# Attention behind a feed-forward block: the last projections, maxima, splits and scales of a batch put at other places of its opening

## What is computed

```python
ckv   = x @ w_kv + b_kv                                   # latent, 128 wide
key   = concat([ckv @ w_ku + b_ku, x @ w_kr + b_kr])      # 256 + 256 wide
q_lat = x @ w_q + b_q
query = concat([q_lat @ w_qu + b_qu, q_lat @ w_qr + b_qr])
value = ckv @ w_vu + b_vu                                 # 512 wide
scores = einsum('bhqd,bhkd->bhqk', heads(query), heads(key))   # 16 heads of 32, causal
at  = softmax(scores / sqrt(32))
out = (at @ heads(value)) @ w_o + b_o
```

## Time and profile before

| | before |
|---|---|
| median of 3 runs | 1224.05 us (1222.79 to 1225.31) |
| the profiled execution, its own time | 1222.3 us |
| its span, first to last instruction | 1220.5 us |
| mean granted TensorE clock | 0.975 |
| TensorE matmuls busy | 1081.9 us (89%) |
| VectorE | 900.7 us (74%) |
| ScalarE | 803.6 us (66%) |
| GpSimd | 362.1 us (30%) |

### The profile page before, as it was taken

The page is one execution under the profiler, slowest core; times in us unless marked ns, Lnnn a source line. Parts: engine busy times, 40 slices in busy tenths (PEclk is TensorE's granted clock), DMA queues, the critical chain, the costliest instruction groups (busy, mean ns, idle before and its releaser), DMA issues.

```text
span 1220.5 us, 18032 instructions
## 1 busy us (share of the span) xinstructions
PE 1081.9 (89%) x5939; PEld 489.4 (40%) x5990; DVE 900.7 (74%) x2229; ACT 803.6 (66%) x1193; POOL 362.1 (30%) x388
## 2 busy tenths in 40 slices
PE   0788999998898789999999699999999799998886
PEld 0343455554444333332344233232344345554443
DVE  4788888989984888884335887884234798888893
ACT  5489888888645345666615355567547988888762
POOL 2101244444561342101210450002200133443456
PEclk9998999998999889999999899999999999999998
DMA  9200000002000221210000321100000000000000
GB/s 368 99 1 1 2 1 1 2 1 57 1 1 1 71 66 29 53 36 2 1 21 9 76 56 34 47 36 2 1 1 1 1 1 19 19 18 18 19 19 35
DMA packets 22287, 37.45 MB, mean 31 GB/s; under 512 B 5398, under 2 KB 7833, under 8 KB 21532
## 3 DMA queue, kind: packets, MB, share of 16 engines
q1 hardware_dynamic: 21404, 34.54, 9.0%
q0 software_dynamic: 768, 1.57, 0.5%
HBM read 19.17 MB, written 4.21 MB: 19 GB/s over the span
## 4 chain that ended last, share of the span: by engine, by line
PE 62%; DVE 21%; issue 7%; SPq 3%; POOL 2%; ACT 2%; DMA 1%; DVEq 1%; another core or an unknown queue 0%; POOLq 0%; ACTq 0%
PE zP L521 14%; PE oP L573 11%; PE xP L693 5%; PE oP L693 5%; PE zP L619 5%; PE zP L677 4%; PE hP L656 3%; PE hP L543 3%; DVE arena L1301 3%; DVE m L1309 3%; PE zP L718 2%; PE hP L718 2%; DVE scored L1506 2%; PE zP L656 2%; DVE arena L1382 1%
## 5 line engine op out<-in xcount | busy, mean ns | idle before, releaser
L834 ACT ACTIVATE arena<-arena,X 128x2048 int8<-128x2048 f32 x154 | 307.9, 2005 | 4.9 <-DVE X L1281 4.8
L893 ACT ACTIVATE arena<-zP,asc 128x512 f32<-128x512 f32 (+3 forms) x384 | 200.6, 582 | 108.2 <-PE zP L681 78.8
L521 PE MATMUL zP<-T,arena 128*128 128x512 f16 x1024 | 249.8, 388 | 0.9
L573 PE MATMUL oP<-T,arena 128*128 128x512 f16 x832 | 200.5, 385 | 0.9 <-DVE arena L1396 0.9
L521 PEld LDWEIGHTS zP<-T,arena 128*128 128x128 f16 x1024 | 102.3, 100 | 123.2 <-issue 12.1
L790 ACT ACTIVATE arena<-zP,sc 128x512 f32<-128x512 f32 x128 | 87.4, 687 | 93.8 <-PE zP L526 65.3
L573 PEld LDWEIGHTS oP<-T,arena 128*128 128x128 f16 x832 | 82.2, 99 | 79.6 <-issue 6.0
L677 PE MATMUL zP<-arena 98*128 98x512 f16 (+3 forms) x384 | 110.5, 334 | 2.6 <-DMA arena<-arena 1.7
L656 PE MATMUL hP<-arena 96*128 96x512 f16 (+3 forms) x256 | 84.0, 351 | 16.0 <-DVE mx L1506 12.9
L1010 POOL TENSOR_SCALAR ln<-ln 128x1 f32<-128x1 f32 x32 | 38.6, 1205 | 189.8 <-DVE ln L1221 189.6
L1506 DVE CUSTOM_DVE_ANT_0 scored<-hP,causal 128x128 bf16<-128x128 f32 (+3 forms) x170 | 80.6, 484 | 19.1 <-PE hP L656 17.8
(11 more groups left out here) (207 smaller groups left out, 1834.6 us busy)
## 6 DMA issues: line engine op xcount, KB each, us to landing
arena<-arena SPq DMA_DIRECT2D x168, 64.0 KB, 2.0
arena<-in_w_synT SPq DMA_DIRECT2D x4, 1024.0 KB, 8.1
arena<-in_w_outT SPq DMA_DIRECT2D x4, 1024.0 KB, 14.8
out_dram<-x_sb SPq DMA_DIRECT2D x16, 256.0 KB, 2.0
x_sb<-in_x SPq DMA_DIRECT2D x3, 1024.0 KB, 14.0
arena<-in_w_o SPq DMA_DIRECT2D x2, 1024.0 KB, 5.0
arena<-arena POOLq DMA_DIRECT2D x24, 64.0 KB, 1.9
arena<-in_b_syn SPq DMA_DIRECT2D x1, 1024.0 KB, 12.0
```

The costliest lines, as they stand in the source:

```text
L521: pe.matmul(zP[:, c * CW:(c + 1) * CW], part[:, g % 2, k, :], T1[:, k, c * CW:(c + 1) * CW], start=(n == 0 and k == 0), stop=False)
L573: mm = pe.matmul(o, part[:, k, :], T2[:, k, :], start=(c == 0 and n == 0 and k == 0), stop=False)
L834: act.activation(junk[:, counted[0] % 2, :], Z[:, g % ZR, :], ACT.Sign, bias=X[:, 2, k:k + 1], accum_out=S[:, k:k + 1]).then_inc(sm["cnt"], 1)
L893: act.activation(PT[:, m // 4 % 2, h, q0:512], colP[m % 3][:, q0:512], ACT.Exp, scale=asc[:, g, 10:11]).then_inc(sm["exp_done"], 1)
```

## The change

It changes the order of work in the opening of a batch. The "in" items for the key planes move forward in `ITEMS`; `project` ends after 14 items; items 14 to 27 stand in `ORDER`, items 14 to 19 among the rows of unit (0, 0) and the values behind them, among the rows of unit (0, 1) (`opening`, `behind_opening`). High halves ("hi"), plane maxima ("peak", with the scales of the group where they complete it) and low halves ("lo") become entries of `ORDER` too. The low halves 0 and 1 come with the first "in 2" item, now the ninth; 2 and 3 are in the opening, 4 to 7 behind eleven rows of unit (0, 1). GpSimd sets the units of stack 0 at the head of `project`, before the first `all_max`; those of stacks 1 and 2 stay. `load_stack` and SyncE's list stay as they are.

```diff
+def opening(rows):
+    order = [("hi", 1), ("item", 14)] + take(4) + [("peak", 14), ("item", 15), ("lo", 2)] + take(4) + [("lo", 3)]
+    order += [("item", 16), ("item", 17)] + take(2) + [("peak", 15), ("item", 18)] + take(2) + [("item", 19)] + take(4)
+    return order
+
+def behind_opening(rows, turn):
+    r = iter(rows)
+    order = [("item", 20), ("item", 21)]
+    for n in range(3):
+        order += [next(r)] + [("item", 22 + n)] * (n < 2)
+    order += [turn, ("item", 24), ("peak", 16), ("peak", 17), next(r), ("item", 25), next(r), ("item", 26), ("hi", 2)]
+    order += [next(r), ("item", 27), ("peak", 18), ("peak", 19), next(r), next(r), ("hi", 3)]
+    for n in range(3):
+        order.append(next(r))
+    for n in range(4):
+        order += [next(r), next(r), ("lo", 4 + n)]
+    return order + list(r)
...
-            others = [[("val", n)] + ([("lo", n + 3)] if 1 <= n <= 4 else []) for n in range(BT)]
-            unit = [e for n in range(BT) for e in others[n] + unit[2 * n:2 * n + 2]]
+            unit = opening(unit)
+        elif (g, qc) == (0, 1):
+            unit = behind_opening(unit, turn)
+            turn = None
...
-        start[u] = min(len(rows), rows.index(("turn", *u)) + 1 + LEAD)
+        lead = [n for n, e in enumerate(rows) if e[0] == "row" and n > rows.index(("turn", *u))]
+        start[u] = lead[LEAD - 1] + 1 if len(lead) >= LEAD else len(rows)
...
         ITEMS = [("in", j, tc) for tc in range(2) for j in (0, 1)]
-        ITEMS += [("up", j, tc) for j in (0, 2, 1, 3, 4, 5) for tc in range(2)]
-        ITEMS += [("in", j, tc) for j in (2, 3) for tc in range(2)]
-        VALUES = len(ITEMS)
+        for kind, j in (("up", 0), ("up", 2), ("in", 2), ("up", 1), ("up", 3), ("in", 3), ("up", 4), ("up", 5)):
+            ITEMS += [(kind, j, tc) for tc in range(2)]
+        assert len(ITEMS) == FIRST_VAL
...
                     evac_item(b, n)
-                    if n - 2 in COMPLETE:
-                        split_hi(b, COMPLETE.index(n - 2))
-                split_hi(b, 3)
+                    if ITEMS[n] == ("in", 2, 0):
+                        split_hi(b, 0)
...
-                            act.wait_ge(sm["p_ps"], (b + 1) * len(ITEMS))
+                            act.wait_ge(sm["p_ps"], b * len(ITEMS) + FIRST_VAL)
...
             def project(b):
+                pool.wait_ge(*((sm["a_rstd"], BT) if b else (sm["x_new"], NT)))
+                unit_rows(b, 0)
                 for g in range(GROUPS):
                     all_max(b, g)
...
             def core(b):
-                for g in range(3):
+                for g in (1, 2):
...
-                for n in range(VALUES):
-                    if not plane(ITEMS[n]):
-                        continue
-                    w, g, tc = plane(ITEMS[n])
+                for n in range(IN_CORE):
+                    if plane(ITEMS[n]):
+                        peak(b, n)
                     if ITEMS[n] == ("in", 2, 0):
-                        for m in range(4):
+                        for m in range(2):
                             split_lo(b, m)
```

More of the change, by code:

```diff
@@ L45, with take @@
 ATT_SCALE = 1.0 / HD ** 0.5
+IN_CORE = 14
+FIRST_VAL = 20
+def opening(rows):
+    r = iter(rows)
+    def take(n):
+        return [next(r) for _ in range(n)]
+    order = [("hi", 1), ("item", 14)] + take(4) + [("peak", 14), ("item", 15), ("lo", 2)] + take(4) + [("lo", 3)]
+    order += [("item", 16), ("item", 17)] + take(2) + [("peak", 15), ("item", 18)] + take(2) + [("item", 19)] + take(4)
+    return order
+def behind_opening(rows, turn):
+    r = iter(rows)
+    order = [("item", 20), ("item", 21)]
[8 more added lines that the diff above has]
+    return order + list(r)
 def core_order():
@@ L295, in program @@
         COMPLETE = [max(n for n, e in enumerate(ITEMS) if plane(e) and plane(e)[1] == g) for g in range(GROUPS)]
-        TOTAL = {k: seen(k, len(ORDER)) for k in ("row", "max", "turn", "col", "mix", "norm", "rec", "mix_v", "val", "lo")}
+        TOTAL = {k: seen(k, len(ORDER)) for k in ("row", "max", "turn", "col", "mix", "norm", "rec", "mix_v")}
         RING = [e for e in ORDER if e[0] in ("row", "turn")]
@@ L318, in x_bank @@
             return hP[:, 0, :] if (f, i) == (1, 0) else xP[:, :]
-        IN_DONE = max(n for n, e in enumerate(ITEMS) if e[0] == "in") + 1
         STACK_OF = (0, 1, 2, 0)
@@ L636, in core @@
                     kind, g = e[:2]
-                    stack = stacks[STACK_OF[g]] if g < GROUPS else None
+                    stack = stacks[STACK_OF[g]] if kind in ("row", "col") else None
                     if kind in ("row", "turn"):
@@ L641, in core @@
                             pe.wait_ge(*free)
[L642 to L645, removed]
+                    elif kind == "item":
+                        item(b, g)
+                    m = n.get(kind, 0)
+                    n[kind] = m + 1
                     if kind == "row":
@@ L878, in core @@
                     kind, g = e[:2]
-                    m = n[kind]
-                    n[kind] += 1
+                    m = n.get(kind, 0)
+                    n[kind] = m + 1
                     if kind in ("row", "turn"):
                         bank, _ = next(ring)
-                    if kind == "val":
-                        evac_item(b, VALUES + g)
+                    if kind == "item":
+                        evac_item(b, g)
+                    elif kind == "hi":
+                        split_hi(b, g)
                     if kind == "col":
@@ L1050, in project, with unit_rows @@
             def project(b):
+                pool.wait_ge(*((sm["a_rstd"], BT) if b else (sm["x_new"], NT)))
+                unit_rows(b, 0)
                 for g in range(GROUPS):
                     all_max(b, g)
+            def unit_rows(b, g):
+                pool.memset(stacks[g][3 * HD:3 * HD + 2, 1, :, :], MUNIT).then_inc(sm["unit_set"], 1)
+                pool.wait_ge(sm["unit_set"], 3 * b + g + 1)
             def all_max(b, g):
@@ L1068, in core @@
                         wait_stack(pool, b, 1)
-                    pool.memset(stacks[g][3 * HD:3 * HD + 2, 1, :, :], MUNIT).then_inc(sm["unit_set"], 1)
-                    pool.wait_ge(sm["unit_set"], 3 * b + g + 1)
+                    unit_rows(b, g)
                 pool.wait_ge(sm["bo_in"], 16 * (b + 1))
@@ L1454, in project, with peak @@
             def project(b):
-                for n in range(VALUES):
-                    if not plane(ITEMS[n]):
-                        continue
-                    w, g, tc = plane(ITEMS[n])
+                for n in range(IN_CORE):
+                    if plane(ITEMS[n]):
+                        peak(b, n)
                     if ITEMS[n] == ("in", 2, 0):
-                        for m in range(4):
+                        for m in range(2):
                             split_lo(b, m)
[L1462 to L1468, removed]
+            def peak(b, n):
+                w, g, tc = plane(ITEMS[n])
+                dve.wait_ge(sm["p_out"], b * len(ITEMS) + n + 1)
+                step(dve.tensor_reduce(mxq[:, g, w, tc:tc + 1], qk[:, w, g, tc * 512:(tc + 1) * 512],
+                                       AX.X, ALU.max, apply_absolute_value=True))
+                if n in COMPLETE:
+                    after(0)
+                    dve.tensor_reduce(asc[:, g, 0:2], mxq[:, g, :, :], AX.X, ALU.max).then_inc(sm["p_max"], 1)
+                    scale(b, g)
             def scale(b, g):
@@ L1498, in core @@
                         split_lo(b, g)
+                    elif kind == "peak":
+                        peak(b, g)
                     if kind == "row":
```

## The result

The changed kernel takes 1226.31 us (median of 20 runs) against 1222.03 us of the kernel before in runs beside it (20 runs): ratio 1.003, 95% interval 1.0016 to 1.0044, so slower by 0.3%. The forecast was +4.75 us on 1224.05; measured were +4.28 us. The profiled execution took 1227.77 us, its span is 1226.0 us, its mean granted clock 0.969.

The account below looks back on a forecast made before the run. TensorE was held to bound the attention, its gaps at each batch opening deciding, with unit (1, 0)'s turn hanging on GpSimd. Shifts of +1.1 and +3.6 us took the profiled 1222.3 to 1227.0; plus 1.75, forecast 1228.8 us, range 1219.5 to 1233.5.

Parts of the forecast that it names:

- the delay that makes up its sum: Memset of stack 2, and behind it GpSimd's additions and turn (1, 0), later by 1.1 us in batch 0, 3.6 in batch 1.
- Maxima of the first unit 17 us earlier, and no gain from it by itself: Batch opening: maxima set at 408.6 against 425.6 before, 17 us earlier; work moved, not saved.
- Lo 7 at 430.8 and 701.2: VectorE's last low half in each opening ends at 430.8 and 701.2, against 420.9 and 689.7 before.
- The rival that it comes sooner: Last low half ends sooner than added up, so no change that can be told, 1224 us; chance 0.25.
- The memset of stack 2 at lo 7 + 10.4 to 11.5: GpSimd starts this memset 10.4 to 11.5 us behind the last low half, taken as 441.8 and 712.2.
- The memset at the front costs nothing and removes a stall: Stack 0's memset at the head of project: first all-reduce 0.4 us late, hidden; L1473's 3.56 us hold goes.
- Either end is before TensorE's next decisive turn and costs nothing there; it only eats the lead.: Unit (0, 1)'s maximum operations inside stack 1's memset: up to 2.2 us, up to 3.5 more for the cast, costing nothing.
- what stood among the rivals for another place: Half clock recurring at the turn of unit (1, 0): up to 2.7 us a batch, 1234 us.
- the ledger: VectorE's work from 384.9 to the last low half: 39.4 us plus 6.4 of waits, without the L1473 stall.
- The turn of (1, 0) hangs on GpSimd's last instruction: VectorE's L1515 comes free only with GpSimd's additions and L1086; TensorE's turn follows 1.45 us behind.
- the sign that the text named as wrong: At the turn of unit (1, 0): VectorE's L1515 taking 0.2 us would show the forecast wrong.
- The chance of 0.16 for the clock or queue overlap on top: Forecast mechanism plus half clock where TensorE is bound (1234 us) or dear overlap of both queues' loads (1233 us); chance 0.16.

Follow-up runs that it names:

- e4: The changed kernel with GpSimd's output bias additions spread, one behind each unit's multiplication, instead of eight ahead of the first: 1223.35 us, ratio 1.0021.
- e2: The kernel before with GpSimd's output bias additions spread, one behind each unit's multiplication, instead of eight ahead of the first: 1219.01 us, ratio 0.9983.
- e9: The changed kernel with the memset of stack 0 back behind the last all-reduce, all of the change but its first step: 1231.64 us, ratio 1.0084.
- e1: The kernel before with only the memset of stack 0 moved to the head of project: 1215.62 us, ratio 0.9951.
- e6: The changed kernel with bias additions spread and GpSimd's memsets of stacks 1 and 2 waiting until unit (0, 1)'s maxima are set: 1215.35 us, ratio 0.9948.
- e5: The changed kernel with GpSimd's memsets of stacks 1 and 2 waiting until the maxima of unit (0, 1) are set: 1214.47 us, ratio 0.994.
- e7: The changed kernel with the four last low halves together, ahead of the rows of unit (0, 1) they stood among: 1209.99 us, ratio 0.99.
- e10: The kernel before with an already satisfied semaphore wait behind each of GpSimd's eight bias additions of a batch: 1220.34 us, ratio 0.9988.

## Why the prediction was right

The time was met, but by luck: its account of where the time goes was half right, and the delay that makes up its sum caused none of the loss (e4 against e2). What was measured is the lock at unit (0, 1) with its half clock, 8.9 to 10.5 us, less the 5 to 6 us that the front memset gave. Neither stands as such in the sum, and their difference happens to be near +4.75.

*Maxima of the first unit 17 us earlier, and no gain from it by itself.* Right: 409.5 less the 1.46 us of offset is 408.1, forecast 407.8, and with all of this reordering in place e9 was slower than before.

*Lo 7 at 430.8 and 701.2.* Right: 431.75 less 1.46 is 430.3; in batch 1, whose first "up" is 2.37 us later than before (650.70 against 648.33), 703.25 less 2.37 is 700.9. The rival that it comes sooner is out.

*The memset of stack 2 at lo 7 + 10.4 to 11.5.* It started at 442.24 (lo 7 + 10.5), and in batch 1 at 709.98 + 7.07 - 3.51 = 713.54 (lo 7 + 10.3, just short of the range). The two memsets ran without a gap, so stack 1 had landed by then. Before, it started at 440.74 and 708.57; each batch in its own frame it came 0.0 and 2.6 us later, forecast 1.1 and 3.6. The additions then began later than before by 0.4 us in batch 0 and 3.4 us in batch 1, each batch in its own frame; expected were 1.1 and 3.6, which batch 1 met.

*The memset at the front costs nothing and removes a stall.* Right, and e1 and e9 put its size at 5 to 6 us. The first all-reduce started at 384.86, in the frame of before 383.4 against 383.31. The Trainium skill ("GPSIMD Engine Reference", on the first call of freshly loaded code) has about 6 us for the load. The trace agrees for this reduce as far as it can tell: it started 6.71 us after the memset's end, but only 0.23 us behind the VectorE reduction that it needs (L1507, which ended at 384.63), so the load was hidden and took 6.71 us at most. The additions, which wait for no engine, started 7.54 us after their memset, and there the page's figure is low.

**The step that failed: "Either end is before TensorE's next decisive turn and costs nothing there; it only eats the lead."** I had the lock at unit (0, 1) with its prices, up to 2.2 us and up to 3.5 more for a caught `cast`, and priced it at nothing because I held the turn of (1, 0) to be decided by GpSimd's additions whatever came before. It wasn't: with the additions gone, e4 was as much slower than e2 as the changed kernel is than the kernel before. The turn of (0, 1) is itself a point where TensorE has nothing else to run: it waited 2.73 and 3.33 us there. With these waits went what stood among the rivals for another place, half clock in a stretch where TensorE is bound: inside them it fell in e4 and in batch 1, and in batch 0 of the changed kernel it had fallen 1.0 us sooner, behind the wait for stack 1, and lasted. By e6 against e4 both together are 8.9 to 10.5 us, more than the whole net loss. What paid for them is the stall that went with the front memset, which the ledger counted only on the way to lo 7 and not as a gain of 3.3 us a batch at the turn.

*The turn of (1, 0) hangs on GpSimd's last instruction.* Half right. In batch 1 it happened as described (3.08 us until the end of L1124, TensorE waiting 1.01 us). In batch 0 the sign that the text named as wrong came true: L1557 at 0.18 us, and no wait of TensorE. By the text's own last sentence the forecast falls where that turn no longer waits for VectorE. The stretch was long there (20.12 us) by the clock: in e4, without the additions, it is 19.68 us. In batch 1 the additions were 1.7 us of it (19.42 against 17.76 in e4), but they had cost 0.8 us there before. The sum came out right, +0.9 and +3.4 for +1.1 and +3.6, with batch 0's term made of other things (0.4 us less up to the turn of (0, 1), 1.3 us more behind it), and within the 1.6 us by which a first stretch varies, so that the agreement of the single batches proves little. Nor was the additions' end as firm a gate as I took it for: in e5 and e7 VectorE got in between them.

The chance of 0.16 for the clock or queue overlap on top was too low for the clock; for the queues it was fair (GpSimd's loads took 6.23 us as before, SyncE's 8.28 us in batch 1 against 8.11, and the first row of group 1, which waits for all of stack 1, started at lo 7 + 10.2).

## What to carry to other kernels

A stall that is "only eating the lead" must be checked against the next point at which TensorE has no other work, not against the next point known to be late: here the two differed, and half clock went with the wait. To learn what a suspect contributes to a change, take it out of both kernels: taken out of the changed one alone, the additions seemed to carry a part of the loss, and they carried none. Long GpSimd instructions belong where VectorE does nothing of the locked kinds; a memset of two partitions made 0.2 us operations last up to 3.5 us. And a change made of several moves should be priced move by move: one alone gave 5 to 6 us, the rest took 10.

## What the hardware showed that was not expected

Of VectorE's operations with both ends in SBUF, not only `tensor_scalar` is held: the `cast` took 3.53 us beside a memset, and the `tensor_tensor` of two SBUF sources 1.20 us beside additions (e5). That the `cast` can be held was only a rule in the prediction; the trace now agrees.

When a held instruction comes free isn't always the end of the instruction that holds it. Between GpSimd's additions, issued back to back, VectorE was let in at the next boundary in some cases (batch 0 of e1, e5 and e9, e7 in both batches) and passed over through two or three boundaries in others: 4.16 and 2.73 us, 3.08 us in the changed kernel, and 3.63 us in e1 batch 1:
```profile
718.14 3.63 DVE L1520 TENSOR_SCALAR mm_<-mm_ 128x16 f32<-128x16 f32 x1
```
That one ended at 721.77, where GpSimd's L1091 ended (720.47 + 1.26 = 721.73). All four came free only at the end of L1086 or the same line of the other kernels, behind which GpSimd waits for that instruction's own semaphore (`link`). With such a wait behind every addition (e10) none of the three held instructions (0.30, 1.14 and 1.24 us) was passed over. Three cases are few, since five others were not passed over without any such wait. The Trainium skill ("SBUF — State Buffer", Who interferes with whom) has the pair of ports locked for one whole instruction; e10 agrees, the four cases show that a wait can last over several. What decides between the two outcomes without a wait stays open.
